# A graph-network kernel on one core: the bias add and the zeroing of the count matrix on GpSimd, and the place of twelve small loads

## The reference

```python
h = jnp.maximum(_layernorm(x, axis=-1), 0.0)
feat_all = jnp.einsum('ni,rhid->rnhd', h, conv_weights)      # 8 relations x 4 heads x 64
el = jnp.sum(feat_all[edge_type, src] * attn_l[edge_type], axis=-1)
er = jnp.sum(feat_all[edge_type, dst] * attn_r[edge_type], axis=-1)
e = leaky_relu(el + er, 0.2)
alpha = softmax of e over the edges of one destination       # segment max, exp, segment sum
x = x + segment_sum(alpha * feat_src, dst) + h_bias          # layer 0
# layers 1 to 3 sum rows over the same edges: the kernel does it with
# a matrix A of counts, A[src, dst] = number of such edges
```

## Time and profile before

| what | value |
|---|---|
| median of three runs | 3207.38 us (3206.33 to 3209.21) |
| the profiled execution, its own time | 3211.49 us |
| its span, first to last instruction | 3209.7 us |
| PE busy | 2858.9 us (89%) |
| DVE busy | 1866.8 us (58%) |
| ACT busy | 1257.0 us (39%) |
| POOL busy | 1017.9 us (32%) |
| one scatter issue on POOL (L523), mean of 499 | 0.987 us |
| one gather issue on POOL (L532), mean of 500 | 0.981 us |
| first scatter issue | at 155.29 us |
| granted TensorE clock, mean | 0.93 |

### The profile page before, as it was taken

How to read it: one execution, slowest core, us unless ns; L and a number is a source line. 1 busy time by engine, 2 the same in 40 slices (tenths; PEclk the granted TensorE clock), 3 DMA queues, 4 the chain that set the end, 5 groups by cost and what they waited for, 6 DMA issues and landing times.

```text
span 3209.7 us, 48246 instructions
## 1 busy us (share of the span) xinstructions
PE 2858.9 (89%) x15034; PEld 1892.2 (59%) x15034; DVE 1866.8 (58%) x5317; ACT 1257.0 (39%) x3665; POOL 1017.9 (32%) x1048
## 2 busy tenths in 40 slices
PE   1789885999999989897788999799999999999998
PEld 1544444999899888887144444455555555545446
DVE  6578884888878766667235433355555555513334
ACT  1122225787778777774004000144444444401000
POOL 3065567777777777776000000000000000000000
PEclk6599986999999999996968999899999999999999
DMA  8966654333333333321843333300000000132232
GB/s 237 402 187 183 194 173 112 101 91 89 89 86 88 89 86 87 88 55 34 299 146 118 102 102 100 106 7 3 7 5 5 7 3 7 38 102 70 83 102 78
DMA packets 245030, 317.60 MB, mean 99 GB/s; under 512 B 121467, under 2 KB 162084, under 8 KB 240740
## 3 DMA queue, kind: packets, MB, share of 16 engines
q1 hardware_dynamic: 191412, 179.07, 19.7%
q0 software_dynamic: 49104, 104.11, 10.9%
q10 hardware_dynamic: 4320, 31.95, 2.5%
HBM read 237.42 MB, written 77.59 MB: 98 GB/s over the span
## 4 chain that ended last, share of the span: by engine, by line
PE 49%; DVE 23%; issue 9%; ACT 5%; POOL 5%; DMA 5%; DVEq 4%; SPq 0%; POOLq 0%
PE PS L1153 17%; PE PS L998 15%; DVE SUMS L1567 4%; DMA BG<-a_d 3%; PE PS L822 3%; PE PS L939 3%; POOL BG L532 3%; PE PS L964 3%; PE PS L977 3%; POOL a_d L523 2%; ACT BG L653 2%; DVE BG L1703 2%; DVEq L1582 2%; DVE OHB L1430 2%; DVE X L1573 1%
## 5 line engine op out<-in xcount | busy, mean ns | idle before, releaser
L523 POOL DMA_INDIRECT a_d<-VAL,IDXS x499 | 492.4, 987 | 241.4 <-issue 135.9
L1153 PE MATMUL PS<-BG,SL 128*128 128x512 f32 (+1 forms) x1440 | 534.7, 527 | 12.2 <-ACT SL L736 12.2
L532 POOL DMA_INDIRECT BG<-feat_d,IDXST x500 | 490.4, 981 | 152.5 <-issue 127.2
L653 ACT ACTIVATE BG<-BG,SL 128x64 f32<-128x64 f32 x2000 | 513.5, 337 | 0.0
L1567 DVE TENSOR_TENSOR SUMS<-SUMS,PS 128x640 f32 x500 | 409.0, 818 | 165.6 <-PE PS L939 153.4
L1153 PEld LDWEIGHTS PS<-BG,SL 128*128 128x128 f32 x1440 | 273.9, 193 | 250.6 <-issue 222.4
L564 POOL MEMSET BG<- 128x7680 f32 x1 | 6.5, 6499 | 1297.1 <-DVE MV L1834 1297.1
L939 PE MATMUL PS<-OHB,BG 128*128 128x128 f32 x2000 | 339.2, 293 | 0.0
L977 PE MATMUL PS<-OHB,X 128*128 128x128 f32 x2000 | 319.5, 283 | 1.7 <-DVEq L1545 1.7
L977 PEld LDWEIGHTS PS<-OHB,X 128*128 128x128 f32 x2000 | 289.7, 197 | 14.7 <-issue 1.7
L964 PE MATMUL PS<-W1A,X 65*128 65x256 f32 x1000 | 276.0, 399 | 3.9 <-ACT X L627 0.9
(11 more groups left out here) (298 smaller groups left out, 4084.2 us busy)
## 6 DMA issues: line engine op xcount, KB each, us to landing
BG<-a_d SPq DMA_DIRECT2D x171, 256.0 KB, 4.2
AL<-a_d SPq DMA_DIRECT2D x137, 256.0 KB, 2.6
a_d<-BG POOLq DMA_DIRECT2D x30, 1088.0 KB, 40.4
feat_d<-SUMS ACTq DMA_DIRECT2D x30, 1040.0 KB, 5.0
BG<-rel_d SPq DMA_DIRECT2D x100, 160.0 KB
X<-in_edge_attr_dram SPq DMA_DIRECT2D x124, 128.0 KB
SUMS<-a_d SPq DMA_DIRECT2D x52, 256.0 KB, 2.6
SL<-key_d SPq DMA_DIRECT2D x50, 256.0 KB
```

What stands on the lines that cost most here:

```text
L523: pool.indirect_dma_start(a_d.rearrange("n (w o) -> (n w) o", o=1), bass.IndirectOffsetOnAxis(ap=IDXS[:, t:t + 1], axis=0), VAL[:, t:t + 1 ...
L532: pool.indirect_dma_start(RING[:, t // NB % 3, t % NB, :], None, feat_d.rearrange("n (r d) -> (n r) d", r=R), bass.IndirectOffsetOnAxis(ap ...
L653: last = act.activation(m, m, ACT.Copy, scale=EXT[:, b % 2, k, 1 + q:2 + q])
L1153: last = pe.matmul(PS[:, to + q, 0:width], lhs[:, i, c, :], w[:, c, q * width:(q + 1) * width], start=(c == 0), stop=(c == kc - 1))
```

## The change

POOL waits for its own memset of ZRO in place of the norm's scale, so the 30 DMAs that zero `a_d` can go out at the start; `zero_ready` now counts the memset and the iota, and DVE waits for both. The bias add moves from DVE to POOL, behind a wait for the bias itself and in front of the write of X to `xb_d`. The twelve D80 loads move on SP's queue from behind the edge arrays to behind the stores of `rel_d` and `key_d`.

```diff
@@ sync
-            for h in range(H):
-                nb = (NS - 1) * NB
-                k = EFULL - nb
-                load(D80[h * NB:(h + 1) * NB, 0:NS - 1, :], dst[0:nb * P].rearrange("(b t e) -> t b e", b=NS - 1, e=P), "dst_in")
-                load(D80[h * NB:h * NB + k, NS - 1, :], ...)
-                load(D80[h * NB + k:h * NB + k + 1, NS - 1, 0:ETAIL], ...)
             load(X[:, 0:NT - 1, :], x[0:(NT - 1) * P, :].rearrange("(t p) d -> p t d", p=P), "x_in")
...
             load(key_d.rearrange("(b t e) -> t b e", b=LB, e=P), KEYT.rearrange("t (b e) -> t b e", b=LB), "key_out")
 
+            for h in range(H):
+                (the same three loads)
+
             sp.wait_ge(s("n0_tp"), NT)
             load(HB, row(h_bias, P), "hb_in")
@@ gpsimd
-            step(pool.memset(ZRO, 0.0))
+            pool.memset(ZRO, 0.0).then_inc(s("zero_ready"), 1)
             pool.iota(TCOL, ...).then_inc(s("zero_ready"), 1)
-            pool.wait_ge(s("norm_scale"), 1)
+            pool.wait_ge(s("zero_ready"), 1)
             for t in range(NT):
                 pool.dma_start(rows(a_d, t)..., bc(ZRO.unsqueeze(1), ...)).then_inc(s("a_zero"), 16)
...
+            pool.wait_ge(s("hb_in"), 16)
+            pool.tensor_tensor(X[:, :, :], X[:, :, :], bc(HB.unsqueeze(1), [P, NT, D]), ALU.add).then_inc(s("x_biased"), 1)
             pool.wait_ge(s("x_biased"), 1)
             pool.dma_start(xb_d.rearrange("(t p) d -> p t d", p=P), X[:, :, :]).then_inc(s("x_out"), 16)
@@ vector
-            dve.wait_ge(s("zero_ready"), 1)
+            dve.wait_ge(s("zero_ready"), 2)
...
-            dve.wait_ge(s("n0_tp"), NT)
-            dve.wait_ge(s("hb_in"), 16)
-            tt(X[:, :, :], X[:, :, :], bc(HB.unsqueeze(1), [P, NT, D]), ALU.add).then_inc(s("x_biased"), 1)
```

More of the change, by code:

```diff
@@ L351, in _ @@
                 load(v[n:n + 1, LB - 1, 0:ETAIL], a[EFULL * P:E].rearrange("(o e) -> o e", o=1), "edges_in")
-            for h in range(H):
-                nb = (NS - 1) * NB
-                k = EFULL - nb
-                load(D80[h * NB:(h + 1) * NB, 0:NS - 1, :], dst[0:nb * P].rearrange("(b t e) -> t b e", b=NS - 1, e=P), "dst_in")
-                load(D80[h * NB:h * NB + k, NS - 1, :], dst[nb * P:EFULL * P].rearrange("(t e) -> t e", e=P), "dst_in")
-                load(D80[h * NB + k:h * NB + k + 1, NS - 1, 0:ETAIL], dst[EFULL * P:E].rearrange("(o e) -> o e", o=1),
-                     "dst_in")
             load(X[:, 0:NT - 1, :], x[0:(NT - 1) * P, :].rearrange("(t p) d -> p t d", p=P), "x_in")
@@ L384, in _ @@
             load(key_d.rearrange("(b t e) -> t b e", b=LB, e=P), KEYT.rearrange("t (b e) -> t b e", b=LB), "key_out")
+            for h in range(H):
+                nb = (NS - 1) * NB
+                k = EFULL - nb
+                load(D80[h * NB:(h + 1) * NB, 0:NS - 1, :], dst[0:nb * P].rearrange("(b t e) -> t b e", b=NS - 1, e=P), "dst_in")
+                load(D80[h * NB:h * NB + k, NS - 1, :], dst[nb * P:EFULL * P].rearrange("(t e) -> t e", e=P), "dst_in")
+                load(D80[h * NB + k:h * NB + k + 1, NS - 1, 0:ETAIL], dst[EFULL * P:E].rearrange("(o e) -> o e", o=1),
+                     "dst_in")
             sp.wait_ge(s("n0_tp"), NT)
```

## The result

The changed kernel took 3269.49 us (median of four runs, 3267.89 to 3277.53) against 3207.84 (3206.33 to 3209.21) for the kernel before on the same chip: ratio 1.0191, 95% interval 1.0169 to 1.0213, +61.7 us. The prediction was 3271. The profiled execution is 3268.38 with a span of 3266.2, 56.5 us more than the span before.

What follows compares the result with a forecast made beforehand. Bound by a chain of waits through DVE to 123 us, then by the rounds' pace. +67 - 6.6 - 12.6 + 16 = +64 us on 3211.49, less 4.1 for the median: 3271 us; eight-in-ten range 3238 to 3290.

Steps and rivals of the forecast that it cites:

- The slip of M: Start of the attention weights (M, L1356): early loads meet the freed zero writes, start at 122 instead of 54.95, +67 us.
- the 18 allowed: From X's landing to a full `conv_in`: 18.8 us, as in the kernel before, with the zeros then gone.
- the lower bound of +61: Start of the attention weights, if engines let strictly equal counts by and the edges' imbalance is absent: `conv_in` at 116, +61.
- The chain behind it: DVE and PE work from L1356 (54.95) to the end of L1402 (123.12), without a load in it: no term in the sum.
- The lock: DVE's L1391 to L1402: if POOL's bias add holds the path, DVE stands for the add's length, +16 us (6.5 to 23).
- The rival without a lock: The bias add on POOL is hidden and holds up no DVE instruction, -16 us: 3255; chance 0.21.
- The add leaves DVE: Before round 0: its copy to VAL follows L1402 by about 7.0 us in place of 13.7, -6.6 us.
- The rounds: Rounds 0 to 4 without zero writes: 14.55 us come back, less 2 us for the write of X, -12.6 us.
- The sum: Whole kernel: +64 us on the profiled 3211.49 is 3275.5; the median lies 4.1 us lower, so 3271 us.

Runs made afterwards that it cites:

- zero_alone: The kernel before with only the zero writes set free at the start; bias add and D80 loads where they were: 3253.97 us, ratio 1.0153.
- zero_x_in: The kernel before with its zero writes waiting for x's arrival in place of the norm's scale: 3266.21 us, ratio 1.0168.
- add_alone: The kernel before with only the bias add moved from DVE to POOL, as one instruction: 3220.07 us, ratio 1.0039.
- split_add: The changed kernel with POOL's bias add cut into 30 adds of one tile each: 3264.97 us, ratio 1.0159 to the kernel before.
- split_late: The kernel before with only the bias add moved to POOL, in 30 adds of one tile each: 3208.69 us, ratio 1.0003.
- spread_add: The kernel before with DVE's bias add cut into 30 pieces between the turned copies, the bias loaded early: 3211.87 us, ratio 1.0008.

## Why the prediction was right, step by step

**The slip of M: +67 predicted, +59.7 measured.** The mechanism, the three late arrivals and their order are as predicted; zero_alone shows that the freed zero writes do it alone, and zero_x_in that the turn is packet for packet. The size is off by 7, in parts that cancel: -17 us for the edges, +3 for X and +7 for the weights. The edges land at 40.0, not 57, since 888 of their packets were through by 10 us (q1's windows from 0), where I had allowed for 400 by 6: q0 passed 31 packets up to 6, 127 from 6 to 8 and 173 from 8 to 10, so that the flood had to build up. The rest of the working holds: of the fullest engine's 348 packets 888 / 5 = 178 were through, and 170 more at 5 / 28 = 0.18 us each are 30 us, an estimate of 40 for the landing. X follows at 89.9, not 104: (89.91 - 40.02) = 49.9 us behind the edges, where the prediction took 47 out of its two sums. From X to a full `conv_in` it took 24.7 us instead of the 18 allowed, because the zeros weren't over (they end at about 107, not 100): what X wins by an earlier start it leaves to the weights. The 18 were themselves misread. The prediction had x in place at about 33 in the kernel before, 9 us early; in zero_x_in, the same kernel up to there, x's load frees POOL at 37.81 only, so that x was about 4 us early and `conv_in` was full some 14 us behind it. The measured slip lies 1.3 us below the lower bound of +61, from strictly equal turns: that bound, and not the middle, was nearly the truth.

**The chain behind it: unchanged.** 57.00 against 57.07, with D80's issues hidden behind it, as predicted. That it would be unchanged was luck in one respect: the prediction took the granted clock of that stage as given, and zero_alone shows that it can be worth 14.5 us.

**The lock: +16 predicted, +14.6 measured.** The add takes 16.34 us (16 taken; 6.5 and 23 the bounds). The GPSIMD Engine Reference's 16.9 by its side-by-side cycle accounting, in the Trainium skill, is an estimate 3% above it. DVE stood for POOL's whole instruction, as add_alone, split_add and split_late show, each in its own way. It cost 1.7 us less than its length because it had begun 1.6 us before DVE's first conversion (170.03 and 171.61). The prediction had it begin behind that conversion: the bias took 3.0 us from its issue at 167.06 to the add, not 5.2. So what stood was not the kind of instruction that the prediction had named, L1391 to L1402 with two inputs in SBUF, but a conversion with one, in the changed kernel and in add_alone both. The rival without a lock (3255) is refuted by the 15.28 us row. The rule of the Trainium skill's SBUF page (Who interferes with whom), whoever starts first blocks the other for the whole instruction, is thereby shown in the direction that the trace of before lacked: 15.28 us of DVE behind 16.34 of POOL, and not only for DVE instructions with two SBUF inputs.

**The add leaves DVE: -6.6 predicted, -3.8 measured.** This term was mis-sized by its mechanism. It charged a key load with 2.5 us, from an undisturbed round, though at this place six of the loads go out within 7.3 us (123.38 to 130.65 in the kernel before) beside zero writes. Rows need 8.06 us from the end of the index adds in spread_add, and 5.67 with the zeros gone in the changed kernel. With the add gone and the zeros left, spread_add gained nothing here; so the 3.8 us come only with the zeros over.

**The rounds: -12.6 predicted, -12.4 measured,** and 3.8 us more from round 4 on that I had not counted, and that no run explains: V4 to V49 is shorter, by 1.7 to 4.0 us, in every kernel that has the add on POOL. That the first number fits is luck: the prediction gave the zero writes 12.6 of the 14.55 us and X's write 2. Zero_alone, which has X's write beside the rounds and no zeros, won 7.0 us only, so that X's write is worth 7.5 by itself. The changed kernel got the other 5.4 because the add, begun early on POOL, let that write land before round 0's copy; in split_add, where it falls into the rounds again, they take 34.41 us instead of 28.42. The add on POOL alone won 10.2 us without touching a zero write, by making DVE late. How much the rounds lose depends on what is left of the zeros and of X's write when they start.

**The sum.** 59.7 - 0.1 + 14.6 - 3.8 - 12.4 - 3.8 = 54.2 us at the last copy to VAL, and 2.3 behind it, make the span's 56.5. The prediction's +64 was 7.5 too high, mostly the slip. That the median came within 1.5 us of 3271 is owed to a second error: I took 4.1 us off because before's profiled execution stood above its median, and the changed kernel's stands 1.1 below its own. So the forecast was right by its mechanism and its largest terms, and closer than these by luck.

**The parts don't add up to the whole.** +46.1, +12.2 and -3.5 make 54.8, and the change costs 61.7. Zero_alone is 14.5 us too good by its clock; with that put back the parts make 69.3, and 7.3 of these are the D80 loads, which cost M that much only where zero writes slow them down. That would fit to 0.3 us, but it counts twice what zero_alone and add_alone both win in rounds 0 to 4 (7.0 and 10.2, where 12.4 are to be had together), so part of the fit is chance.

Left open: why the clock rose in zero_alone and stayed low in every other profile without the added multiplications. With them it rises each time as far as the record shows: their three kernels were profiled once each, with 1.00 in the stage, and all their 29 executions have a mean granted clock of 0.937 to 0.943, where the 57 of the kernel before beside the experiments have 0.928 to 0.935.

## What to carry to other kernels

Work that nobody waits for isn't free to start early: on shared DMA engines each packet of another queue costs yours about one turn, so before freeing a large write, count the packets (not the bytes) of every load that it will meet, down to the smallest weights: in zero_x_in these cost 57 us. Before moving an operation off the critical engine, look at what it hides there; here it hid loads and cost nothing, and in its new place it held the same engine for 15 us through the other one's hands. And read the granted clock of each stage: the 38 us at 0.50 held more to win here (9.4 us won, and perhaps 6 more) than any part of the change.

## What the runs showed of the hardware that was not expected

- Two queues pass packets one for one even when one side's hold 4.1 KB and the other's about 11 bytes (0.07 MB / 6338): 99 of each per us, where small ones alone go at 1458 per us (4375 in 3 us).
- PE, busy for all of 33 us with fp32 work of 128 and 64 columns, was left at 0.50 (1.2 GHz); with 28 multiplications of 512 columns run ahead of it, where PE had been idle, the same work ran at 1.00 (2.4 GHz) from its start, 22.1 us in place of 38.3, or 28.9 with the wait for the 28.
- Splitting the pattern of a write, or the write itself, into quarters of 2176 bytes didn't make packets of 2176 bytes: those of 2 KB and more stayed at 4.35 KB, and four times as many DMAs only added packets of under 512 bytes (607 in place of 165 in 32 us).
- A POOL add of 128x256 takes 0.717 us beside an idle DVE, against 0.54 per tile in one piece of 7680, and a median of 1.137 us while DVE works on SBUF, whose instructions mostly grow by 0.4 us each: both engines pay for the turns.
